# Additive mask of an attention block: from ScalarE copies into two reserved PSUM banks to one fp32r matmul per score tile in a common turn of eight banks

## The reference

```python
x = x + tanh(g_xattn) * attention(layernorm(x), ctx, ctx, mask, Wq, Wk, Wv, Wo)   # 16 heads of 64
x = x + tanh(g_ffn)   * experts(layernorm(x), Wg, bg, W1, b1, W2, b2)             # 8 experts, top 2
# inside attention, for sequence b and head h:
scores = qh[b, h] @ kh[b, h].T + mask[b, 0]       # 64 x 64, one mask for all 16 heads
probs  = softmax(scores); out = probs @ vh; then @ Wo
# inside experts: relu(x @ W1[e] + b1[e]) @ W2[e] + b2[e], weighted by the renormalized top-2 gates
```

## Time and profile before

| | |
|---|---|
| runs (3), median | 1113.28 us (1110.3 to 1116.44) |
| profiled execution | 1110.3 us |
| its span | 1108.6 us |
| PE busy | 1017.1 us, 92% |
| DVE busy | 936.0 us, 84% |
| ACT busy | 901.6 us, 81% |
| POOL busy | 794.1 us, 72% |
| DMA queue of all loads and moves | 23.4% of the DMA engines' time |

### The profile page before, as it was taken

One profiled execution on the slowest core, in us unless ns is written; L12 is line 12 of the kernel. 1 busy time (PEld: TensorE's weight loads), 2 busy tenths in 40 slices (PEclk: granted clock), 3 DMA queues, 4 the chain that ended last, 5 costly groups with the idle time before them and its releaser, 6 DMA issues.

```text
span 1108.6 us, 36239 instructions
## 1 busy us (share of the span) xinstructions
PE 1017.1 (92%) x13797; PEld 755.7 (68%) x13797; DVE 936.0 (84%) x1899; ACT 901.6 (81%) x1681; POOL 794.1 (72%) x719
## 2 busy tenths in 40 slices
PE   5878899999999999999999989999999999999896
PEld 4456676767767677676777767676776767777664
DVE  3797888888989988898988978988898898888777
ACT  2999787888878888787978878888887888888765
POOL 3677676786768778676777758678676877779853
PEclk9999999999999999999999999999999999999999
DMA  9123311222222122222222222122222212222100
GB/s 218 40 49 74 66 38 40 54 54 52 48 59 50 40 52 56 50 49 51 53 42 52 53 49 47 41 56 52 52 47 59 50 30 44 46 40 51 20 11 20
DMA packets 123162, 56.90 MB, mean 51 GB/s; under 512 B 26584, under 2 KB 122864, under 8 KB 122992
## 3 DMA queue, kind: packets, MB, share of 16 engines
q1 hardware_dynamic: 122992, 54.59, 23.4%
HBM read 16.80 MB, written 4.19 MB: 19 GB/s over the span
## 4 chain that ended last, share of the span: by engine, by line
PE 49%; DVE 13%; issue 11%; POOL 11%; ACT 9%; DVEq 0%; ACTq 0%; POOLq 0%
PE bank L44 15%; PE bank L46 14%; PE bank L45 14%; POOL hidL L882 3%; POOL ptL L919 3%; POOL rstd L867 3%; PE bank L306 2%; DVE x2hat L654 2%; PE bank L261 2%; ACT pt L568 2%; ACT bank L510 2%; DVE comb L855 1%; DVE above L831 1%; POOL x L914 1%; ACT vH L548 1%
## 5 line engine op out<-in xcount | busy, mean ns | idle before, releaser
L882 POOL TENSOR_TENSOR hidL<-hid,hidH 128x512 f16<-128x512 f32 x242 | 279.7, 1168 | 18.8 <-ACT hidH L493 18.7
L919 POOL TENSOR_TENSOR ptL<-pt,ptH 128x512 f16<-128x512 f32 x128 | 149.1, 1165 | 142.1 <-ACT pt L568 141.9
L483 ACT ACTIVATE hid<-bank,b1col 128x512 f32<-128x512 f32 x256 | 183.4, 716 | 39.5 <-PE bank L46 39.0
L463 ACT ACTIVATE qH<-bank 128x512 f16<-128x512 f32 x256 | 154.9, 609 | 54.4 <-PE bank L46 53.4
L493 ACT ACTIVATE hidH<-bank,b1col 128x512 f16<-128x512 f32 x256 | 185.7, 725 | 0.0
L44 PE MATMUL bank<-w2H,hidH 128*128 128x128 f16 x1024 | 180.7, 221 | 5.4 <-DVE hidL L775 4.7
L662 DVE TENSOR_TENSOR qL<-bank,qH 128x512 f16<-128x512 f32 x224 | 152.8, 682 | 34.8 <-ACT qH L463 33.0
L45 PE MATMUL bank<-w2L,hidH 128*128 128x128 f16 x1024 | 180.6, 221 | 0.0
L46 PE MATMUL bank<-w2H,hidL 128*128 128x128 f16 x1024 | 180.5, 221 | 0.0
L925 POOL TENSOR_TENSOR prob<-prob,row_inv 128x512 f32<-128x512 f32 x128 | 133.6, 1044 | 63.2 <-DVE row_inv L769 63.2
L914 POOL TENSOR_TENSOR x<-x,y_scaled 128x512 f32<-128x512 f32 x114 | 146.2, 1282 | 13.7 <-DVE x L733 13.7
(11 more groups left out here) (142 smaller groups left out, 3586.6 us busy)
## 6 DMA issues: line engine op xcount, KB each, us to landing
vdH<-vH SPq DMA_DIRECT2D x256, 64.0 KB, 2.1
vdL<-vL SPq DMA_DIRECT2D x256, 64.0 KB, 2.1
x_raw<-in_x SPq DMA_DIRECT2D x16, 256.0 KB, 3.0
ctx_raw<-in_ctx SPq DMA_DIRECT2D x16, 256.0 KB, 3.2
mask_raw<-in_fside_Bx1xSxS SPq DMA_DIRECT2D x32, 128.0 KB, 2.9
out_x<-x SPq DMA_DIRECT2D x16, 256.0 KB, 2.5
qH<-in_L_xattn_Wq SPq DMA_DIRECT2D x1, 512.0 KB, 5.8
qH<-in_L_xattn_Wk SPq DMA_DIRECT2D x1, 512.0 KB, 8.5
```

Of the source, the lines that this page charges most:

```text
L463: act.activation(qH[:, g % 2, 2 * j + g2, :, h2, :], bk("Q", g, h)[:, :].rearrange("p (b q) -> p b q", b=GB), ACT.Copy).then_inc(s_q_high, 1)
L483: act.activation(hid[:, k % NR, :], bk("hid", g, e, c)[:, :], ACT.Relu, bias=b1col[:, e, c:c + 1]).then_inc(s_relu[c], 1)
L882: pool.tensor_tensor(hidL[:, m % 2, c, :], hid[:, k % NR, :], hidH[:, m % 2, c, :], ALU.subtract).then_inc(s_hid_low[c], 1)
L919: pool.tensor_tensor(ptL[:, b % 2, :], pt[:, b % 2, :], ptH[:, b % 2, :], ALU.subtract).then_inc(s_pt_low, 1)
```

## The change

PE now adds the mask. DVE builds a constant `spread` once: a 128 x 128 matrix of four 64 x 64 blocks, each 32 times the identity, of type fp32r. For each group DVE splits the mask, whose rows lie twice in SBUF (partitions 0 to 63 and 64 to 127): a CAST of all 128 partitions to fp32r, and a subtraction on partitions 64 to 127 that leaves there what the rounding took off. One fp32r matmul with `spread` as weights and the split mask, repeated eight times, as the moving operand then writes high part plus low part, times 32, into the whole score bank, and the three passes accumulate on it. `mask_into_bank` and the two first matmuls are gone. Scores take their bank from a common turn of all eight banks. The raw mask has one buffer in place of two, and its load waits for DVE's subtraction.

```diff
-        score_bank, turn = bank[:NSCORE], bank[NSCORE:]
+            if kind == "scores":
+                return [(s_shift, at[0] + 1)]
...
         def take_bank(*name):
-            bank_of[name] = turn[len(taken) % len(turn)]
+            bank_of[name] = bank[len(taken) % NBANK]
             taken.append(name)
-            return evicted(taken[-1 - len(turn)]) if len(taken) > len(turn) else []
+            return evicted(taken[-1 - NBANK]) if len(taken) > NBANK else []
...
             def scores(b):
-                pe.wait_ge(s_mask_in, b + 1)
+                for freed in take_bank("scores", b):
+                    pe.wait_ge(*freed)
...
+                    pe.wait_ge(s_mask_low, g + 1)
+                dst = bk("scores", b)
+                pe.matmul(dst[:, :].rearrange("p (j k) -> p j k", j=JG), spread[:, :],
+                          mask_parts[:, g % 2, i, :].unsqueeze(1).to_broadcast([P, JG, S]),
+                          start=True, stop=False, skip_group_check=True)
...
-            for b in range(NSCORE):
-                last = pe.matmul(score_bank[b][:, :], wq_raw[:, 0, :], wk_raw[:, 0:4, :].rearrange("p h d -> p (h d)"),
-                                 start=True, stop=True)
-            last.then_inc(s_marked, 1)
...
-                if within(s + 1, B):
-                    mask_into_bank(s + 1)
...
+                if i == 5 - sooner and within(g + 1, GROUPS):
+                    parts = mask_parts[:, (g + 1) % 2, :, :]
+                    dve.wait_ge(s_mask, 32 * (g + 2))
+                    if g >= 1:
+                        dve.wait_ge(s_scores, GB * g)
+                    dve.tensor_copy(parts, mask_raw[:, :, :]).then_inc(s_mask_high, 1)
+                    dve.wait_ge(s_mask_high, g + 2)
+                    dve.tensor_tensor(parts[S:P], mask_raw[S:P, :, :], parts[S:P], ALU.subtract).then_inc(s_mask_low, 1)
...
             def load_mask(g):
-                if g >= 2:
-                    sp.wait_ge(s_mask_in, GB * (g - 1))
                 if g >= 1:
-                    sp.wait_ge(s_mask, 32 * g)
+                    sp.wait_ge(s_mask_low, g)
```

More of the change, by code:

```diff
@@ L19 @@
 NBANK = 8
-NSCORE = 2
 TILES = B // 2
@@ L60, in flamingo_block @@
         ident = sb("ident", [P, P])
+        spread = sb("spread", [P, P], F32R)
         tri = sb("tri", [P, E, E])
@@ L76, in flamingo_block @@
         ctx_raw = sb("ctx_raw", [P, 2, GT, D])
-        mask_raw = sb("mask_raw", [P, 2, GB, S])
+        mask_raw = sb("mask_raw", [P, GB, S])
+        mask_parts = sb("mask_parts", [P, 2, GB, S], F32R)
         stats = sb("stats", [P, 2, GT, 6])
@@ L158, in flamingo_block @@
             sem(n) for n in ("b1col", "tanh", "logitT_out", "gate_exp", "pickedT_high"))
-        s_wdve, s_scale = sem("weights_low"), sem("out_scale")
+        s_wdve, s_spread, s_scale = sem("weights_low"), sem("spread"), sem("out_scale")
         s_xT_low, s_ctxT_low, s_x2T_low = sem("xT_low"), sem("ctxT_low"), sem("x2T_low")
@@ L165, in flamingo_block @@
         s_scaled, s_b2_add, s_y_tail, s_hid_tail = (sem(n) for n in ("y_scaled", "b2_add", "y_add_tail", "hid_low_tail"))
-        s_marked, s_mask_in = sem("score_banks_marked"), sem("mask_in_bank")
+        s_mask_high, s_mask_low = sem("mask_high"), sem("mask_low")
         s_ln = [{k: sem(f"ln{w}_{k}") for k in ("stats", "aggr", "var", "rows")} for w in range(2)]
@@ L287, in scores @@
                 cols = slice(i * S, (i + 1) * S)
-                pe.wait_ge(s_mask_in, b + 1)
+                for freed in take_bank("scores", b):
+                    pe.wait_ge(*freed)
+                if b == 0:
+                    pe.wait_ge(s_spread, 1)
                 if i == 0:
@@ L292, in scores @@
                     pe.wait_ge(s_ctxT_low, g + 1)
-                dst = score_bank[b % NSCORE]
+                    pe.wait_ge(s_mask_low, g + 1)
[3 more added lines that the diff above has]
+                          start=True, stop=False, skip_group_check=True)
                 for jg in range(JG):
@@ L361, in _ @@
             pe.wait_ge(s_load["Wk"], 16)
-            for b in range(NSCORE):
-                last = pe.matmul(score_bank[b][:, :], wq_raw[:, 0, :], wk_raw[:, 0:4, :].rearrange("p h d -> p (h d)"),
-                                 start=True, stop=True)
-            last.then_inc(s_marked, 1)
             for n in range(H // 4):
-                for freed in take_bank("weights", n):
-                    pe.wait_ge(*freed)
+                take_bank("weights", n)
                 for i in range(4):
@@ L377, in _ @@
                     at = H // 4 + 2 * k + n
-                    for freed in take_bank("weights", at):
-                        pe.wait_ge(*freed)
+                    take_bank("weights", at)
                     for i in range(4):
@@ L500, in transposed_high @@
                 act.activation(high, bk(name, g)[:, :], ACT.Copy).then_inc(count, 1)
[L502 to L512, removed]
             for n in range(H // 4):
@@ L669, in softmax_src @@
             def softmax_src(b):
-                return score_bank[b % NSCORE][:, :].rearrange("p (j k) -> p j k", j=JG)
+                return bk("scores", b)[:, :].rearrange("p (j k) -> p j k", j=JG)
+            dve.wait_ge(s_ident, 1)
+            for half in (slice(0, S), slice(S, P)):
+                for col in (slice(0, S), slice(S, P)):
+                    last = dve.tensor_scalar(spread[half, col], ident[half, half], WS, None, ALU.mult)
+            last.then_inc(s_spread, 1)
             ln_stats(0, 0, x_raw[:, 0], x_loaded(0))
@@ L963, in load_mask @@
             def load_mask(g):
-                if g >= 2:
-                    sp.wait_ge(s_mask_in, GB * (g - 1))
                 if g >= 1:
-                    sp.wait_ge(s_mask, 32 * g)
+                    sp.wait_ge(s_mask_low, g)
                 for half in range(2):
-                    sp.dma_start(mask_raw[half * S:(half + 1) * S, g % 2, :, :],
+                    sp.dma_start(mask_raw[half * S:(half + 1) * S, :, :],
                                  mask[GB * g:GB * (g + 1), 0].rearrange("b q k -> q b k")).then_inc(s_mask, 16)
```

## The result

The changed kernel takes 1155.82 us (median of four runs, 1152.26 to 1157.04), beside 1114.86 us for four runs of the kernel before: a ratio of 1.0367 (95% interval 1.0324 to 1.041). The forecast was 1131 us with a range up to 1148. The direction was right, the size was not: the profiled execution grew by 45.5 us where the sum said 18.3. Three executions (the profiled one of e3, one of e8, one of the kernel before beside e3) lasted about two to three times as long as the others of their kernel; the medians are taken with them, the ratios without.

A forecast was written before the change was run, and what follows sets the result against it. PE, busy 92% of the span, was taken as the bound. Groups +24.3, start -3.5, attention-only part -1.5 and end -1 sum to +18.3 us on the 1113.3 median: 1131 us predicted, own range 1122 to 1140, full range 1109 to 1148.

The forecast's parts named there:

- c: PE time of one 512-column fp32r mask matmul, taken as 0.23 us; eight in a group make 1.84 us.
- R2: Rival: the mask matmul runs at the pace of fp32 transposes, 0.46 us each, giving 1150 us; chance 0.13.
- A: PE's 0.79 us wait for the residual add at i = 2, claimed to go with the common turn of banks.
- M: Mask cast and subtraction on DVE between xhat and L647, semaphore included: 1.15 us, ends 0.9 and 1.7.
- A second effect of the delay: POOL's break beside x2hat on DVE at i = 6 goes, so x2hat takes 0.86 us more.
- R1: Rival: no third disturbed part of x2hat, so 11.2 us go: +7.1, 1120 us; chance 0.17.
- B: PE's wait for the residual add at i = 6, 2.71 us before, claimed to become 3.53 us.
- A group thus costs 1.87 us more: Per group: 1.84 us of matmuls, less 0.79, plus 0.82 for the two residual-add waits; 13 groups make +24.3 us.
- The start: The two fp32 matmuls go, so PE's first product starts at 10.25 in place of 13.80: 3.5 us gained.
- The attention-only part: Gains from ACT without mask copies, against three mask splits on DVE: together -1.5 us, ends -5 and +3.
- The end: Last group without a next mask, about -0.3 us, and experts' tail gaining some 0.7: -1 us.
- R3: Rival: the split costs nothing at i = 5, since shorter ACT steps start its chain 1.3 us earlier; 1103.5 us, chance 0.15.

The follow-up runs named there:

- e3: The changed kernel with the mask split done for the first group only and used for all groups: 1102.89 us, ratio 0.9878.
- e8: The changed kernel with the split at the end of i = 3 and x2hat moved behind the residual add of i = 6: 1109.8 us, ratio 0.9951.
- e1: The changed kernel with the first hidden half at i = 6 done four times more ahead of the residual-add wait: 1134.57 us, ratio 1.0172.
- e2: The changed kernel with the split at the end of i = 6, behind the residual add (first mask's at i = 3): 1123.99 us, ratio 1.0077.
- e7: The kernel before, with nine more matmuls at i = 6 behind the residual-add wait: 1147.27 us, ratio 1.0284.
- e6: The changed kernel with the mask split at the end of i = 3: 1135.43 us, ratio 1.0185.
- e10: The changed kernel, split kept at i = 5, with x2hat moved behind the residual add of i = 6: 1120.42 us, ratio 1.0037.
- e9: The kernel before with x2hat moved behind the residual add of i = 6: 1090.47 us, ratio 0.9774.
- e5: The kernel before, with the cast and subtraction added on DVE at i = 5 into a tile nothing reads: 1163.87 us, ratio 1.043.

## Why the prediction was wrong

By its own steps:

- *One matmul per score tile*, c = 0.23: measured 0.25. Right; R2 (0.46) is out.
- *The common turn of eight banks*: A is gone, nothing else came late. Right.
- *ACT without the mask copies* buys nothing in the steady part. Right: ACT is busy 51.3 us of a group in place of 54.7, and now waits for PE.
- *Two DVE instructions*, M = 1.15: measured 1.17. The sum is right, in part by luck: from its start to the next start the cast takes 0.45 us where 0.52 was taken, the subtraction 0.72 where it was 0.63 with the semaphore.
- *A second effect of the delay*, 0.86: x2hat takes 3.77 us with its third part disturbed. Right; R1 is out.
- *B after the change*, 3.53: measured 3.60. Right.
- *A group thus costs 1.87 us more*: **this is the step that failed.** It adds up waits and work as if PE worked behind a wait of 3.5 us at the pace of before. It didn't: its clock fell to 1.2 GHz for 3.4 or 6.8 us. The group costs 4.1 us more than an undisturbed one of before. Of the 2.24 us that this is beyond the forecast, e1 takes 1.77 away by filling the wait; 0.47 are left, of which c gives 0.16 and B 0.07, and 0.24 I could not locate. The factor of 13 was also one too high for B: in the thirteenth group it didn't grow.
- *The start* gained 3.4 us as said (the first product of Q at 23.12 us, before at 26.50). *The attention-only part* gave it back: in the changed kernel three stretches of 6.8 us at half clock, in e2, where PE idles 1.99, 2.38 and 2.75 us at these places in place of 2.00, 2.40 and 3.93 us, one of 3.4, and there group 4's xhat starts at 171.2 us, 4.3 us earlier than before. The forecast's -5.0 is near that. That the clock alone makes the difference isn't shown, since e2 has its splits at another place.
- *The end*: +5.9 where +2.7 was summed; it has a B and two stretches at half clock too.

The books over the 11 steady groups: forecast +20.6; the 0.47 makes +5.2; half clock after the change +19.4 (11 x 1.77); and 5.9 us go off because the kernel before had three stretches and one B of 3.8 us of its own there, which my group of 65.22 us did not contain. Sum 39.3; it must come out as measured, since the 0.47 is what was left over.

The Trainium skill (TensorE: Matmul & The Clock Gate, "HAM oscillation — how this bites in real kernels") describes a loop in which each wait for data throws the clock back, so that the price is paid in every round. The traces here agree: 12 waits of 3.6 us, 12 stretches at 0.50. Waits of 2.7 us brought one only in some rounds (2 of 11 before). By that rule the forecast would have needed a rival "B brings half a clock in every group": the 1.6 us of one short stretch before, 13 times, less the ones already there, gives about 1131 + 16 = 1147 us, and with some long stretches more.

R3, the faster case, failed where it was said that it would: DVE waits for nothing on the chain of B but POOL's rstd, so no earlier start came. R3's 1103.5 us is reached by e3 (1102.89), which has no split behind the first group's.

What stays open: which waits of about 2.5 to 3 us bring the half clock. The kernel before has it at 2 of 11 waits of 2.7 us, e7 at 7 of 11, e6 at 10 of 11 of 2.99 us. In the steady part waits of 2.05 us and less (e10) and one of 2.26 us (e9) had none, those of 3.6 us and more had it always. In the attention-only part shorter ones had one too: in the changed kernel PE idled 1.11 us from 32.8 us on and 2.00 us from 34.5 us on, and its clock was at half from 35.4 us on.

## What to carry to other kernels

A wait on PE costs more than its length once the clock falls behind it, so before summing, read the granted clock in the slices right behind each large wait, in several periods and not in the cleanest one, and give the stretch at half clock a term of its own. A chain that ends in such a wait is the worst place for new work, however short: 1.1 us of DVE work there cost 3.4 us of each steady group in e5 (69.12 beside 65.76 us). Moving work on the same engine to an earlier step helps only if that engine waits for something in between; look for that idle time first, or take another engine.

## What the runs showed of the hardware that I had not expected

- Stretches at half clock last 3.4 or 6.8 us in every trace here (but for the one in which an execution ends), and in the steady part of the changed kernel they begin between 0.9 us ahead of the wait's end and 0.6 us behind it.
- Twelve idle-filling matmuls, together 2.6 us, ahead of a wait in each of 13 groups made the kernel 21 us faster than it was without them.
- An fp32r matmul of 512 columns costs PE 0.25 us though its record lasts 0.58, about that of fp16 (0.21).
- A DVE cast of 128 x 512 to fp32r takes 0.42 us beside an idle POOL and 1.16 to 1.39 us beside a busy one; the subtraction of 64 x 512 takes 0.69 and 1.53 us. So the price of the same work more than doubles with its place.
